# Layer 0's expert down products in three one-pass products, the last two units closed by batch halves, and a new order

## What is computed

```python
xn = layernorm(x)
s = attention0(xn)                                   # 16 heads of 16
gate, value = silu(xn @ w1[e]), xn @ w2[e]           # 8 experts, 256 -> 128
g = sum over the token's two best e of p_e * ((gate * value) @ w3[e])   # 128 -> 256
x = x + s * silu(g)
xn = layernorm(x)
# layer 1: per value head a 128 x 128 state
#   delta = (v_t - k_t S) b_t ;  S = d_t S + k_t delta ;  o_t = q_t S
o = rmsnorm(o) * norm_w * silu(xn @ Wz.T)
x = x + (o @ W_out.T) * silu(moe1(xn))
```

## Time and profile before

| | |
|---|---|
| median of 3 runs | 1293.44 us |
| the profiled execution | 1291.24 us |
| its span, first to last instruction | 1288.1 us |
| PE / DVE / ACT / POOL busy | 1246.8 / 1086.3 / 912.3 / 907.4 us |
| layer 0's experts and attention | about 30 to 220 us |
| layer 1's units | about 260 to 1285 us |

### The profile page before, as it was taken

How to read it: one execution, slowest core, us unless ns; L and a number is a source line. 1 busy time by engine, 2 the same in 40 slices (tenths; PEclk the granted TensorE clock), 3 DMA queues, 4 the chain that set the end, 5 groups by cost and what they waited for, 6 DMA issues and landing times.

```text
span 1288.1 us, 33126 instructions
## 1 busy us (share of the span) xinstructions
PE 1246.8 (97%) x12248; PEld 1066.1 (83%) x12248; DVE 1086.3 (84%) x2385; ACT 912.3 (71%) x2537; POOL 907.4 (70%) x1179
## 2 busy tenths in 40 slices
PE   8999999899999999999999999999999999999996
PEld 7656455678889898989898889899999989989895
DVE  5887466899698998999999888988888879888887
ACT  4001654597878787887878888788787888787784
POOL 4121533757797778758787888887888789887664
PEclk9887999899999999999999999999999999999997
DMA  7921101222110111111111113122212221321221
GB/s 231 250 74 47 36 30 62 82 46 75 23 53 25 41 34 46 27 35 34 59 43 42 31 53 101 42 65 65 71 55 71 66 84 44 84 73 48 74 67 46
DMA packets 59771, 81.66 MB, mean 63 GB/s; under 512 B 6300, under 2 KB 44316, under 8 KB 59612
## 3 DMA queue, kind: packets, MB, share of 16 engines
q1 hardware_dynamic: 54876, 65.26, 18.5%
q0 software_dynamic: 4736, 14.29, 4.0%
HBM read 66.69 MB, written 12.71 MB: 62 GB/s over the span
## 4 chain that ended last, share of the span: by engine, by line
PE 68%; DVE 17%; ACT 7%; issue 4%; POOL 2%; DMA 2%; SPq 0%; POOLq 0%; DVEq 0%; ACTq 0%
PE ps L1112 26%; PE ps L1460 3%; PE ps L1474 3%; PE ps L1444 3%; PE ps L1403 3%; PE ps L1413 3%; PE ps L1416 2%; PE ps L1445 2%; DVE yv L1861 2%; PE ps L1470 2%; DVE ZL L1970 2%; PE ps L1383 2%; PE ps L1174 2%; PE ps L1297 2%; PE ps L1218 2%
## 5 line engine op out<-in xcount | busy, mean ns | idle before, releaser
L2225 ACT ACTIVATE XY<-ps 128x512 f16<-128x512 f32 x384 | 221.1, 602 | 88.4 <-PE ps L1416 86.5
L1970 DVE TENSOR_TENSOR ZL<-ps,cst 128x256 f16<-128x256 f32 x384 | 152.4, 415 | 21.9 <-PE ps L1403 21.0
L1861 DVE SCALAR_TENSOR_TENSOR yv<-ps,cw,yv 128x511 f32<-128x511 f32 (+2 forms) x192 | 142.3, 743 | 9.4 <-ACT yv L2169 6.6
L1112 PE MATMUL ps<-XH,WVh 128*128 128x256 f32 (+1 forms) x384 | 132.8, 346 | 0.5 <-ACT st L2273 0.3
L1112 PE MATMUL ps<-XH,WVl 128*128 128x256 f32 (+1 forms) x384 | 122.7, 319 | 0.0
L1112 PE MATMUL ps<-XL,WVh 128*128 128x256 f32 (+1 forms) x384 | 122.3, 319 | 0.0
L1413 PE MATMUL ps<-ZL,XY 128*128 128x64 f16 x1536 | 104.1, 193 | 0.8 <-DVE ZL L1970 0.4
L1416 PE MATMUL ps<-XY,ZL 128*128 128x64 f16 x1536 | 104.0, 193 | 0.0
L1403 PE MATMUL ps<-XY,LT 128*128 128x64 f16 x1536 | 95.5, 193 | 2.5 <-ACT XY L2225 2.4
L2259 ACT ACTIVATE sq<-O 128x128 bf16<-128x128 f32 x256 | 79.3, 310 | 26.0 <-DVE O L2020 12.0
L1403 PEld LDWEIGHTS ps<-XY,LT 128*128 128x128 f16 x1536 | 77.1, 98 | 19.2 <-issue 9.2
(11 more groups left out here) (329 smaller groups left out, 4355.2 us busy)
## 6 DMA issues: line engine op xcount, KB each, us to landing
RC<-crow SPq DMA_DIRECT2D x128, 128.0 KB
WV<-in_WV SPq DMA_DIRECT2D x16, 512.0 KB, 3.5
exr<-in_ex SPq DMA_DIRECT2D x16, 384.0 KB, 3.2
WK<-in_WK SPq DMA_DIRECT2D x16, 256.0 KB, 2.8
WO<-in_WO SPq DMA_DIRECT2D x16, 256.0 KB, 3.2
rows_out<-st SPq DMA_DIRECT2D x7, 512.0 KB, 4.9
KS<-spread SPq DMA_DIRECT2D x12, 256.0 KB, 8.4
QS<-spread SPq DMA_DIRECT2D x12, 256.0 KB, 12.0
```

Source lines behind the costliest of these rows:

```text
L1112: m = pe.matmul(o, a, b, start=c + k == 0, stop=c == 1 and k == 2)
L1861: m = dve.scalar_tensor_tensor(out=dst[:, k:512], in0=ps[:, bk, 0:512 - k], scalar=cw[:, h, j, 3 - k:4 - k], in1=dst[:, k:512], op0=ALU.mu ...
L1970: leave(dve.tensor_tensor(half(ZL[:, k - 2], k, 0), p, lv(k), ALU.mult), "a", u, k)
L2225: leave(act.activation(changed(u, k), ps[:, bank("b", u, k), :].rearrange("p (c n t) -> p c n t", c=2, t=1 << (k - 1)), ACT.Copy), "b", u, k)
```

## The change

Three edits and a new order.

1. `exd` becomes three one-pass products for each of the old ones. `split_expert` now splits all 768 columns, and a new part `eh` makes the two halves of hT0: ACT copies it rounded into hTh, POOL subtracts into hTl. `exd` waits for that.
2. For the units 62 and 63 (TAIL) `sq`, `on`, `ot`, `os` and `y` are made by batch, two lanes at a time. `pf` on DVE closes all earlier units' yacc into st before the last products are there; the last `y` of a tile is then multiplied by `total` on its way out of ps, and `fin` adds it. SP writes a tile out as soon as its last addition is done.
3. In every `y` the eight products that need only OGH come before the four that need OGL, and PE waits for OGL only between them.
4. RANK and LATER have new numbers throughout, so every queue's order is new.

```diff
@@ RANK, LATER (two lines of some 120)
-    "KS": {"ACT": -143.99, "DVE": 15.75, "PE": -171.35}, "KS:first": {"ACT": -30.89, "DVE": 105.49, "PE": -151.3},
+    "KS": {"ACT": 70.91, "DVE": 34.08, "PE": -117.9}, "KS:first": {"ACT": -9.41, "DVE": -47.09, "PE": -92.22},
...
@@ run_tensor
                 elif what == "exd":
                     e, b, q = x[1:]
                     k = 8 * b + e
                     bk = enter(*x)
-                    w.wait_ge(d_ex[k % 3], 16 * (k // 3 + 1))
-                    w.wait_ge(*done("exv", e, b))
+                    w.wait_ge(s_exs, k + 1)
+                    w.wait_ge(s_el, nth("POOL", "eh", e, b))
                     for n in (2 * q, 2 * q + 1):
-                        m = pe.matmul(ps[:, bk, 256 * (n % 2):256 * (n % 2) + 256],
-                                      hT0[:, k % 3, 128 * n:128 * n + 128], exr[:, k % 3, 512:768],
-                                      start=True, stop=True)
+                        at = slice(128 * n, 128 * n + 128)
+                        for j, (a, c) in enumerate(((hTh, exh), (hTh, exl), (hTl, exh))):
+                            m = pe.matmul(ps[:, bk, 256 * (n % 2):256 * (n % 2) + 256], a[:, k % 3, at],
+                                          c[:, k % 3, 512:768], start=j == 0, stop=j == 2)
...
+                elif what == "y" and x[1] in TAIL:
+                    u, b = x[1:]
+                    h = u // 4
+                    bk = enter(*x)
+                    w.wait_ge(s_wo, h + 1)
+                    w.wait_ge(s_ogh, nth("POOL", "os", u, b))
+                    for v in range(2):
+                        for k, weights in enumerate((WOh, WOl)):
+                            pe.matmul(ps[:, bk, 0:256], OGH[:, 2 * b + v, :], weights[:, h % 2, v, :],
+                                      start=v + k == 0, stop=False)
+                    w.wait_ge(s_ogl, nth("POOL", "os", u, b))
+                    for v in range(2):
+                        m = pe.matmul(ps[:, bk, 0:256], OGL[:, 2 * b + v, :], WOh[:, h % 2, v, :], start=False, stop=v == 1)
                     signal(m, *x)
...
@@ run_vector
                 elif what == "fin":
-                    i = x[1]
-                    w.wait_ge(*done("y", NU - 4 + i))
+                    i, b = x[1:]
+                    n = 4 * b + i
+                    w.wait_ge(*done("y", NU - 4 + i, b))
+                    dve.tensor_tensor(st[:, n, :], st[:, n, :], yacc[:, n, :], ALU.add).then_inc(s_fx, 1)
+                elif what == "pf":
+                    i, b = x[1:]
+                    n, u = 4 * b + i, NU - 4 + i
+                    w.wait_ge(*done("y", u - 4 if u in TAIL else u))
                     w.wait_ge(d_xb, 16)
-                    w.wait_ge(s_fs, 2)
...
+                    w.wait_ge(s_fs, nth("ACT", "fs", b))
+                    dve.tensor_tensor(yacc[:, n, :], total[:, n, :], yacc[:, n, :], ALU.mult).then_inc(s_fm, 1)
+                    w.wait_ge(s_fm, nth("DVE", *x))
+                    dve.tensor_tensor(st[:, n, :], st[:, n, :], yacc[:, n, :], ALU.add).then_inc(s_px, 1)
...
+                elif what == "y" and x[1] in TAIL:
+                    u, b = x[1:]
+                    i, n = u % 4, 4 * b + u % 4
+                    w.wait_ge(*full(*x))
+                    w.wait_ge(s_px, nth("DVE", "pf", i, b))
+                    leave(dve.tensor_tensor(yacc[:, n, :], ps[:, bank(*x), 0:256], total[:, n, :], ALU.mult), *x)
...
@@ run_scalar
+                elif what == "eh":
+                    e, b = x[1:]
+                    k = (8 * b + e) % 3
+                    w.wait_ge(*done("exv", e, b))
+                    act.activation(hTh[:, k, :], hT0[:, k, :], ACT.Copy).then_inc(s_eh, 1)
...
@@ run_gpsimd
-                split(exr[:, k % 3, 0:512], exh[:, k % 3, :], exl[:, k % 3, 0:512], s_exh, s_exs, k + 1)
+                split(exr[:, k % 3, :], exh[:, k % 3, :], exl[:, k % 3, :], s_exh, s_exs, k + 1)
...
+                elif x[0] == "eh":
+                    e, b = x[1:]
+                    k = (8 * b + e) % 3
+                    w.wait_ge(s_eh, nth("ACT", *x))
+                    pool.tensor_tensor(hTl[:, k, :], hT0[:, k, :], hTh[:, k, :].bitcast(F32), ALU.subtract).then_inc(s_el, 1)
...
+                elif x[0] == "os" and x[1] in TAIL:
+                    u, b = x[1:]
+                    two = slice(2 * b, 2 * b + 2)
+                    w.wait_ge(*done("ot", u, b))
+                    w.wait_ge(*full("y", u - 1, *((b,) if u - 1 in TAIL else ())))
+                    split(O[:, u % 2, two], OGH[:, two], OGL[:, two], s_ogh, s_ogl, nth("POOL", *x))
```

265 lines of the change are left out of this document (152 added, 113 removed), and 22 rows, old and new, of the table RANK.

## The result

The changed kernel is slower: median 1296.72 us (22 runs, 1291.31 to 1303.06) against 1292.09 for the kernel before (22 runs, 1288.41 to 1295.80). The ratio is 1.0034, with a 95% interval from 1.0023 to 1.0046: 4.4 us more, where 4.9 us of gain were forecast. Timed once more later (e12) the ratio was 1.0017 (1.0002 to 1.0032).

What follows compares the result with a forecast made beforehand. The units were taken as bound by the number and length of PE's instructions. Terms -4.2 + 1.3 + 1.0 + 0.5 + 1.0 - 4.5 = -4.9 gave 1288.5 us from a median of 1293.44; range 1281.5 to 1295.0.

Steps and rivals of the forecast that it cites:

- the price of the products: Layer 0's down products on PE: three one-pass products take 0.357 us instead of 0.443, saving 0.086 for each of 64.
- the softmax: Layer 0's softmax: POOL's and ACT's added work fits beside it; 2.75 us of the down products' saving counted in full.
- +1.3: First experts: ACT's copy and POOL's subtraction delay the first down product to about 39.6; +1.3 us, from 0 to +4.
- -4.2: Layer 0's one-pass down products: 2.75 us saved in batch 1's softmax, 1.4 among batch 0's row maxima; between -2.5 and -8.
- +1.0: Layer 0: fetches of experts 3 to 5 about 4.4 us later, plus the wider split; +1.0 us, from 0 to +5.
- the masks: Layer 0's softmax: PE's products wait for masks queued behind POOL's wider splits; +0.5 us, bound +5.
- -4.5: Last units: turning and gating by halves ends 6.1 us earlier, less collisions; -4.5 us, between -7.5 and -1.5.
- the 1.6 taken off: Last units: one and a half overlaps of DVE's closings with POOL's splits, 1.6 us off the end's gain.
- The end gives little: Rival: DVE's closings before unit 63's gating collide with POOL's splits four times; end -1.5 instead of -4.5, 1291.5 us; chance 0.18.
- The units, "+1.0": The units' new order: 13 more returns of PE from f16 to float32 work; +1.0 us, from -3 to +4.
- the first rival: The new order packs PE better than the count says: gain of 3 instead of loss of 1, 1283.1 us; chance 0.14.
- layer 0's dependence on POOL: Rival: ACT and POOL before the down products delay layer 0, deciding above 8 us of delays; 1296.0 us; chance 0.13.

Runs made afterwards that it cites:

- e12: The changed kernel timed again, unaltered, with a second profiled execution: 1297.22 us, ratio 1.0017 to the kernel before.
- e1: The changed kernel with its new order, but layer 0's down products in their old float32 form: 1295.78 us, ratio 1.0015 to the kernel before.
- e2: The kernel before with only the end changed (last two units by batch halves, high products first): 1290.87 us, ratio 0.9983.
- e3: The kernel before with only the down products changed to three one-pass products, PE, DVE and SP in the old order: 1321.33 us, ratio 1.0223.
- e6: The changed kernel with a filler product (48 rows, 512 columns) ahead of each of the 64 row-maxima blocks: 1319.58 us, ratio 1.0206 to the kernel before.
- e14: The changed kernel with a filler product (128 rows, 256 columns) ahead of each of the 64 row-maxima blocks: 1293.93 us, ratio 0.9985 to the kernel before.
- e16: The changed kernel without eight closing multiplications by the shared scale in the last units' preparation: 1294.85 us, ratio 0.9995 to the kernel before.
- e7: The changed kernel without POOL's subtraction for hTl; the third down product reads hTh instead: 1293.90 us, ratio 1.0016 to the kernel before.
- e4: The changed kernel with DVE's negations of the row maxima moved right behind the last maximum: 1294.21 us, ratio 1.0009 to the kernel before.
- e11: e3 without POOL's low part of hT; the third product reads the high part again: 1297.87 us, ratio 1.0019 to the kernel before.
- e9: The kernel before's order up to unit 60, with old down products, then the changed kernel's order with halved last units: 1293.74 us, ratio 0.9986.
- e13: e2 with a filler product (128 rows, 256 columns) ahead of each of the 64 row-maxima blocks: 1290.25 us, ratio 0.9966 to the kernel before.
- e15: e2 with only the last unit in halves, unit 62 as before: 1294.13 us, ratio 0.9978 to the kernel before.
- e17: e9 with the filler product of 128 rows ahead of each row-maxima block: 1291.24 us, ratio 0.9977 to the kernel before.

## Why the prediction was wrong

**Right: the price of the products, the start, the softmax.** The timeline of the changed kernel at the first experts, against the earlier trace rows:

```profile
39.10 0.35 PE L1219 MATMUL ps<-exh,hTh 128*128 128x256 f32 x1 [1.24 <-POOL hTl L2441]
...
39.29 0.28 PE L1219 MATMUL ps<-exl,hTh 128*128 128x256 f32 x1
...
39.41 0.28 PE L1219 MATMUL ps<-exh,hTl 128*128 128x256 f32 x1
...
40.86 3.19 SPq L987 DMA_DIRECT2D exr<-in_ex  x3
...
52.42 0.82 POOL L2382 CAST exh<-exr 128x768 fp32r<-128x768 f32 x1 [10.96 <-DMA exr<-in_ex]
53.32 1.80 POOL L2384 TENSOR_TENSOR exl<-exr,exh 128x768 fp32r<-128x768 f32 x1
```

Down products step 0.12 us at the upper clock, three to a product as forecast. The first stood at 39.10 (39.6 forecast), after a wait for POOL of 1.24; the first row maxima came 0.9 to 1.7 us later (+1.3). POOL has 35 us more (942.4 in all). PE never waited for POOL's masks, and the softmax became 1.7 us shorter. The fetch behind the first experts was issued 4 us later, at 40.86, and landed 2.5 later, with 1.1 us of wait for the split. The splits last 0.82 and 1.80; I had 0.92 and 1.92. That these terms came out doesn't carry the sum: each was priced at a place where little hung on it.

**The step that failed: layer 0, "-4.2", "+1.3" and "+1.0" together.** Their sum was -1.4 with the masks; layer 0 took +8.8 in a typical execution. The step that failed is that the new order of layer 0 stood in the sum at nothing, and that the down products' saving and delays were priced as if they met the old order. Three parts:

1. *The order of layer 0: some 5 us.* I compared the two orders in the units alone. In layer 0 I priced each edit in its old surroundings, as if the rest stood still. With the old products and the new order layer 0 is 5.0 us longer, and the median 4.9 us higher (e1 against e2, one chip). The place is the handover. From the last maxima to the first scores the old order takes 11.6 to 12.1 us in every trace but e3's (15.2), whether 0 or 41 us of layer 0 lay at 1.2 GHz. The new order takes 19.2 in e1, because DVE negates the maxima 9.0 us behind the last of them instead of 1.4: it first finishes batch 0's last expert, and the transposes on PE wait for it. Of these 7.5 us a part is work that was only brought forward (PE is busy for 15.2 of the 19.2 us, and for 11.1 of 11.7 before).
2. *The dependence on POOL, elsewhere than I looked: some 3 us.* I counted its latency at the first experts and the masks. It came at batch 0's last expert, 2.95 us ahead of the row maxima's turn, and then in DVE's four small steps beside POOL's wider splits, 4.9 us instead of 0.8. Not all of this is the new step's: e1 has a wait of 3.0 us for the same negations and 1.3 for the hidden rows, so 4.2 of the 8.5 us of waits are. The handover grows from 19.2 us to 21.4 to 22.8, in the five traces with the changed kernel's layer 0 (both of its own, e6, e14, e16). Without POOL's step it is 19.7 (e7), with the negations moved ahead 19.4 (e4). The collision with POOL I had seen for the end and not looked for here. The page "SBUF — State Buffer", section "Who interferes with whom", of the Trainium skill says that VectorE's copies and tensor-scalar steps, where they run in a two-port mode, also exclude GpSimd for a whole instruction. The rows of 128.20 and 130.70 agree: 0.19 and 0.20 us alone, 1.68 and 1.82 beside subtractions of 1.82 and 1.80.
3. *The clock: not separated.* I took the stretch at 1.2 GHz as given. The changed kernel's runs have 8 to 10 us more of it than before. At the 0.32 us of span that go with each from run to run, that would be 2.6 to 3.2 us, an estimate; it overlaps with the first two, since PE's waits of part 2 are followed by a stretch at 0.50 (130 to 135 us).

And the -4.2 itself was too large. e11 has the products without POOL's turn and is not faster than before. In the softmax, where I counted 2.75 us in full, the new products take 1.4 us off in the new order (104.8 in e1, 103.4 in the changed kernel) and nothing in the old. Of batch 0's half nothing shows; that DVE's maxima and the waits hide it is my reading and wasn't tried by itself.

**The end, "-4.5": right within its own stretch, wrong for the kernel.** From unit 63's state to the end the changed kernel takes 15.8 us, 4.3 less than before. But I held that state's time fixed. The four steps that were put before it (3.1 us) sit on a DVE that was 94% busy, and the state comes 2.8 to 3.0 us later; from unit 60 on the gain is 1.3 to 1.5 us. e9 shows this without the rest of the new order. The halves add their own steps: DVE has 38.1 us of work instead of 34.1 from unit 60 on. The chain of the changed kernel's end runs through DVE, closing by closing; here from 1291.8 us on:

```profile
1291.80 0.42 DVE L1989 TENSOR_TENSOR xt<-total,xt 128x256 f32<-128x256 f32 x1
1292.25 0.42 DVE L1991 TENSOR_TENSOR st<-st,xt 128x256 f32<-128x256 f32 x1
1292.60 0.42 DVE L1989 TENSOR_TENSOR xt<-total,xt 128x256 f32<-128x256 f32 x1
1293.05 0.43 DVE L1991 TENSOR_TENSOR st<-st,xt 128x256 f32<-128x256 f32 x1
1293.39 0.74 DVE L2097 TENSOR_TENSOR O<-ps,Z 128x256 f32<-128x256 f32 x2
```

Unit 63's gating (L2097, 1293.39) stands behind six closing instructions in a row, of which the last four are shown. Three of the closing steps met POOL's subtractions: L1989 took 0.94 us at 1286.21, L1991 0.84 at 1294.58, L1982 0.79 at 1295.99, instead of 0.41 to 0.43. That is 1.3 us, near the 1.6 taken off. POOL's power I had at 1.31 us for two columns, from one record. Its mean over the 64 of four columns is 1.04 before, and two columns take 0.72 to 0.87 in the changed kernel, so that term was too high. "The end gives little" was the rival that held, for another reason than its own.

**The units, "+1.0".** From layer 0's end to unit 60: -1.4 and -2.1. From there to unit 63's state it is +2.8 to +3.0, which belongs to the end's account. Within the range, but of the other sign: over all traces the new order's units take 1013.1 to 1016.8 us and the old one's 1015.9 to 1022.5. The count of returns from f16, 13 more, told nothing that can be seen. So the first rival, a better-packed order, held in the units and failed in layer 0.

**The rival that came nearest** was layer 0's dependence on POOL, 1296.0 us. That its number is so near is luck. Its place was half right and its working wrong: its three delays came to some 4 us, below the 8 from which it was to decide, while the order and the turn of the row maxima, which it did not name, made the rest.

**Which version is faster than both.** The end alone: 0.9983, and 0.9966 with the filler of e13. Both intervals end below 1, and so do those of e9, e15 and e17. These are gains of 0.1 to 0.3%, too small to rank the five. The down products in three are not worth having here in any order that was tried.

**What stays open:** why the clock falls where it does. PE was busy for 20.00 of 20 us in the stretch at 0.50. A filler of 128 rows and 256 columns kept it up, one of 48 rows and 512 columns did not; rows, columns and operands differ at once, so the runs don't say which of them did it. Open too is whether the new order lengthens the time at 1.2 GHz ahead of the handover; the handover itself hardly varies within either order. Why units in the old order take longer on two of the chips wasn't looked into.

## What to carry to other kernels

Price an edit of one engine's work at the place where that engine is about to run dry, the last item before a turn, and not only at the first one; then ask what shares a port with the small steps of that turn. Where a chain at the end is shortened by putting work of a nearly full engine ahead of it, measure from a point before that work, or the gain is counted that another stretch pays. When a search gives a new order along with an edit, run the order without the edit: here that one run moved more than the edit. And put milestones on both sides of a turn from one stage to the next: the handover was the same within 1.5 us in each order, where whole times scattered by ten, and it showed what the order did.
